# Reordering the activation slab by time then channel in a two-layer spatio-temporal network on one core

## The reference

```
x_res = conv2d(swapaxes(x, 1, 2), res_w, res_b)
xc = swapaxes(_attention(swapaxes(x, 1, 2), W1_c, W2_c, True), 1, 2)    # over channels
xt = swapaxes(_attention(swapaxes(xc, 1, 3), W1_t, W2_t, True), 1, 3)   # over times
s  = _attention(xt, W1_s, W2_s, False)                                  # over nodes
h  = einsum('bnm,bmct->bnct', s * A[None], xt)
g  = einsum('bnct,cf->bnft', h, W_gcn)
y  = relu(conv2d(swapaxes(g, 1, 2), tcn_w, tcn_b, pad 1) + x_res)
z  = (y - mean over channels) / sqrt(var + 1e-05) * ln_g + ln_b
```

## Time and profile before

| | us |
|---|---|
| median of 3 runs | 2099.84 |
| span of the profiled execution | 2096.6 |
| PE busy | 1603.6 (76%) |
| DVE busy | 1216.3 (58%) |
| ACT busy | 716.1 (34%) |
| POOL busy | 489.9 (23%) |

### The profile page before, as it was taken

The page is one execution under the profiler, slowest core; times in us unless marked ns, Lnnn a source line. Parts: engine busy times, 40 slices in busy tenths (PEclk is TensorE's granted clock), DMA queues, the critical chain, the costliest instruction groups (busy, mean ns, idle before and its releaser), DMA issues. The chain is left out here.

```text
span 2096.6 us, 28757 instructions
## 1 busy us (share of the span) xinstructions
PE 1603.6 (76%) x8438; PEld 1232.3 (59%) x8438; DVE 1216.3 (58%) x2496; ACT 716.1 (34%) x1145; POOL 489.9 (23%) x854
## 2 busy tenths in 40 slices
PE   4589799999655279999999333788999999147776
PEld 4439577777433168888888233276777777135554
DVE  4511277787645844444444377121677877658986
ACT  3302144434334033333332122021344344047775
POOL 1100033443501231111110365000234434201111
PEclk7599799999879579999999655888999999579988
DMA  6403012212156133333331777033122111012322
GB/s 198 118 17 104 23 46 60 68 53 60 46 173 197 42 117 117 117 116 116 116 117 43 221 237 228 15 111 103 33 61 63 57 60 49 27 48 81 90 76 67
DMA packets 151973, 193.44 MB, mean 92 GB/s; under 512 B 11657, under 2 KB 103273, under 8 KB 151917
## 3 DMA queue, kind: packets, MB, share of 16 engines
q1 hardware_dynamic: 101021, 116.46, 19.0%
q10 hardware_dynamic: 41680, 47.96, 7.3%
q0 software_dynamic: 9216, 28.32, 4.5%
HBM read 126.64 MB, written 66.06 MB: 92 GB/s over the span
## 5 line engine op out<-in xcount | busy, mean ns | idle before, releaser
L701 PE MATMUL g_y<-L_z,L_pt 128*128 128x192 f32 x1024 | 188.6, 327 | 0.3 <-ACT L_pt L917 0.2
L909 ACT ACTIVATE L_e<-g_s,L_nm 128x512 f32<-128x512 f32 x128 | 88.0, 687 | 287.1 <-DVE L_nm L745 286.3
L701 PEld LDWEIGHTS g_y<-L_z,L_pt 128*128 128x128 f32 x1024 | 170.8, 190 | 1.2 <-ACT L_pt L917 1.2
L865 POOL TENSOR_TENSOR L_xr<-L_xr,L_lnb 128x192 f32<-128x192 f32 x128 | 84.8, 690 | 306.1 <-DMA L_xr<-x 159.9
L1193 POOL DMA_INDIRECT x_xin<-xn_rows,x_index x64 | 66.3, 1036 | 295.3 <-PE ex_t L1207 146.8
L872 POOL TENSOR_TENSOR L_t<-L_rstd 128x48 f32<-128x48 f32 x96 | 35.6, 371 | 320.1 <-DVE L_rstd L806 315.1
L668 PE MATMUL g_z<-L_kw,L_xnT 96*128 96x192 f32 x512 | 95.8, 341 | 15.1 <-DVE L_v L775 15.1
L1287 DVE TENSOR_TENSOR x_mid<-ex_g,x_sig 128x480 f32<-128x480 f32 (+1 forms) x48 | 31.4, 654 | 122.4 <-ACT x_sig L1362 122.4
L668 PEld LDWEIGHTS g_z<-L_kw,L_xnT 96*128 96x128 f32 x512 | 86.5, 196 | 27.0 <-DVE L_v L775 27.0
L754 DVE SCALAR_TENSOR_TENSOR L_p<-L_e,L_rl,L_adj 128x512 f32<-128x512 f32 x128 | 96.4, 753 | 4.7 <-DVE L_rl L752 0.3
L745 DVE TENSOR_REDUCE L_nm<-g_s 128x1 f32<-128x512 f32 x128 | 87.9, 686 | 13.4 <-PE g_s L677 7.9
(11 more groups left out here) (267 smaller groups left out, 4005.5 us busy)
## 6 DMA issues: line engine op xcount, KB each, us to landing
xn_rows<-L_xnT SPq DMA_DIRECT2D x48, 384.0 KB, 3.8
L_xnT<-xn_rows SPq DMA_DIRECT2D x48, 384.0 KB, 3.4
y_slots<-x_yo ACTq DMA_DIRECT2D x64, 240.0 KB, 2.4
x<-L_y ACTq DMA_DIRECT2D x32, 384.0 KB, 3.2
L_xa<-in_x SPq DMA_DIRECT2D x16, 384.0 KB, 4.1
L_raw<-xn_rows SPq DMA_DIRECT2D x16, 384.0 KB, 3.4
L_xr<-in_x SPq DMA_DIRECT2D x16, 384.0 KB, 3.3
L_xa<-x SPq DMA_DIRECT2D x16, 384.0 KB, 4.0
```

Source lines behind the costliest of these rows:

```text
L701: last = nc.tensor.matmul(out, pt[k % 2][:, P * c:P * c + P], z[q][:, c, :], start=False, stop=(c == NK - 1))
L865: last = nc.gpsimd.tensor_tensor(v_, v_, gain(s.lnb), ALU.add)
L909: nc.scalar.activation(e[k % 2][:, :], pss[k % 2][:, :], ACT.Exp, bias=s.nm2[:, k % 2:k % 2 + 1], accum_out=s.l[:, k % 2:k % 2 + 1]).then_ ...
```

## The change

All slabs are ordered by time, then channel: a column is time * 16 + channel. The host lays x out so before the launch, and the kernel writes its output back in the old order. In parts:

1. `small_attention` reads contiguous columns for both attentions. The channel fold becomes the same for both halves (one matmul and one copy where there were two), the time fold differs (two matmuls and one copy twice as wide).
2. `mix_channels` has one 96 x 96 block for both halves. Each of the 8 matmuls of an item has 96 columns and doesn't accumulate. It writes its half in channel-time order, as the time attention wants it.
3. `graph_conv`: the residual weights are 96 columns wide, so the two matmuls have 97 rows and 96 columns each; the projections have 96 weight columns; `u` and `v` have 128 rows, cleared by four DVE operations at the start of the stage; the slab copy goes from DVE to ACT, where it stands ahead of the exponential; the sums over channels read contiguous elements; POOL's four operations with `ln_b` and four with `ln_g` are one each.
4. `route` counts in the old token order: six matmuls for each choice instead of two, running sums over 16 items instead of 32 half items, and one more addition.
5. `feed_forward` writes its sum to new buffers `yo` in channel-time order; the wait for an earlier store moves from DVE's product to POOL's addition.
6. `conv_weights` and the constants follow the new order (masks per half, 96 columns of residual weights, ones for both halves).

```diff
@@ small_attention
-    xa = s.shared[:, 0:B * NK * CT].rearrange("p (b k c t) -> p b k c t", b=B, k=NK, c=C)
+    xa = s.shared[:, 0:B * NK * CT].rearrange("p (b k x w) -> p b k x w", b=B, k=NK, w=W)
...
-                        rhs = xa[:, :, k, :, x] if chan else xa[:, :, k, x, :]
-                        last = nc.tensor.matmul(psp[0:PROJ, 0:n_all], w[:, k, x, :], rhs,
+                        last = nc.tensor.matmul(psp[0:PROJ, 0:n_all], w[:, k, x, :], xa[:, :, k, x, :],
                                                 start=(j == 0), stop=(j == n - 1))
@@ mix_channels
-                        for h in range(2):
-                            last = nc.vector.tensor_tensor(
-                                big[z % 2][0:HALF, h, :].rearrange("p (c t) -> p c t", t=T),
-                                s.rct[0:HALF, h, bass.ds(b * C, C)].unsqueeze(2).to_broadcast([HALF, C, T]),
-                                s.tmask[:, 1, :].unsqueeze(1).to_broadcast([HALF, C, T]), ALU.mult)
-                        last.then_inc(big_done, 1)
+                        nc.vector.tensor_tensor(
+                            big[z % 2][0:HALF, 0, 0:HALF].rearrange("p (c t) -> p c t", t=TH),
+                            s.rct[0:HALF, bass.ds(b * C, C)].unsqueeze(2).to_broadcast([HALF, C, TH]),
+                            s.tmask[:, 0, 1, 0:TH].unsqueeze(1).to_broadcast([HALF, C, TH]),
+                            ALU.mult).then_inc(big_done, 1)
...
-                                last = nc.tensor.matmul(psm[z % 2][:, k // 2, CT * (k % 2):CT * (k % 2) + CT],
-                                                        xnT[z][0:HALF, h, P * k:P * k + P], big[z % 2][0:HALF, h, :],
-                                                        start=(h == 0), stop=(h == 1))
+                                last = nc.tensor.matmul(
+                                    psm[z % 2][:, k // 2, CT * (k % 2):CT * (k % 2) + CT].rearrange(
+                                        "p (c t) -> p c t", t=T)[:, :, TH * h:TH * h + TH],
+                                    xnT[z][0:HALF, h, P * k:P * k + P],
+                                    big[z % 2][0:HALF, 0, 0:HALF].rearrange("p (c t) -> p c t", t=TH),
+                                    start=True, stop=True)
@@ graph_conv
-        oct_ = lambda t: t[:, :, :].rearrange("p k (o t) -> p k o t", t=T)
-        lanes = lambda t: t.unsqueeze(2).to_broadcast([P, NK, O, T])
-        gain = lambda t: t[:, :].rearrange("p (o x) -> p o x", x=1).to_broadcast([P, O, T])
+        oct_ = lambda t: t[:, :, :].rearrange("p k (t o) -> p (k t) o", o=O)
+        flat = lambda t: t[:, :, :].rearrange("p k t -> p (k t)")
+        lanes = lambda t: flat(t).unsqueeze(2).to_broadcast([P, NK * T, O])
+        gain = lambda t: t[:, :].unsqueeze(1).to_broadcast([P, NK * T, O])
...
-                        last = nc.tensor.matmul(psz[0:NPROJ, 1, :], kw[q][0:HALF, h, 0:NPROJ], xnT[q][0:HALF, h, :],
+                        last = nc.tensor.matmul(psz[0:HALF, 1, :], kw[q][0:HALF, h, 0:HALF], xnT[q][0:HALF, h, :],
...
-                    nc.tensor.matmul(pss[k % 2][:, :], u[q][0:KR, P * k:P * k + P], v[q][0:KR, :],
+                    nc.tensor.matmul(pss[k % 2][:, :], u[q][:, P * k:P * k + P], v[q][:, :],
...
-                    nc.tensor.matmul(out, xnT[q][0:HALF + 1, 0, P * k:P * k + P], s.res[0:HALF + 1, 0, :],
-                                     start=True, stop=False)
-                    nc.tensor.matmul(out, xnT[q][0:HALF, 1, P * k:P * k + P], s.res[0:HALF, 1, :],
-                                     start=False, stop=False)
+                    for h in range(2):
+                        nc.tensor.matmul(out[:, HALF * h:HALF * h + HALF], xnT[q][0:HALF + 1, h, P * k:P * k + P],
+                                         s.res[0:HALF + 1, h, :], start=(h == 0), stop=False)
...
+                for padded in (*u, *v):
+                    nc.vector.memset(padded[:, :].bitcast(F32), 0.0)
...
-                def copy_z(b, q):
-                    dve.wait_ge(z_done, ready(b))
-                    dve.wait_ge(y_done, free(b, 2))
-                    nc.vector.tensor_copy(slab(z[q]), psz[:, :, 0:2 * CT]).then_inc(z_sb, 1)
...
-                    step(nc.vector.tensor_reduce(s.mu[:, :, :], y[q][:, :, :].rearrange("p k (o t) -> p k t o", t=T),
-                                                 AX, ALU.add))
+                    step(nc.vector.tensor_reduce(flat(s.mu), oct_(y[q]), AX, ALU.add))
...
-                        copy_z(b + 1, r)
                         row_max(b + 1, 0)
...
-                        for k in range(NK):
-                            v_ = dv[q][:, k, :].rearrange("p (o t) -> p o t", t=T)
-                            last = nc.gpsimd.tensor_tensor(v_, v_, gain(s.lng), ALU.mult)
-                        last.then_inc(gained, 1)
+                        nc.gpsimd.tensor_tensor(oct_(dv[q]), oct_(dv[q]), gain(s.lng), ALU.mult).then_inc(gained, 1)
...
+                def copy_z(b, q):
+                    act.wait_ge(z_done, ready(b))
+                    act.wait_ge(y_done, free(b, 2))
+                    nc.scalar.activation(slab(z[q]), psz[:, :, 0:2 * CT], ACT.Copy).then_inc(z_sb, 1)
...
                     if project:
+                        copy_z(b + 1, r)
                         row_exp(b + 1, 0)
@@ feed_forward
-                        nc.gpsimd.tensor_tensor(ya[q][:, :, :], ya[q][:, :, :], xr[q][:, :, :],
-                                                ALU.add).then_inc(out_done, 1)
+                        in_time = lambda t: t[:, :, :].rearrange("p k (t c) -> p k t c", c=C)
+                        pool.wait_ge(sent[q], dma_free(i))
+                        nc.gpsimd.tensor_tensor(yo[q][:, :, :].rearrange("p k (c t) -> p k t c", t=T),
+                                                in_time(ya[q]), in_time(xr[q]), ALU.add).then_inc(out_done, 1)
```

More of the change, by code:

```diff
@@ L36 @@
 HALF = CT // 2
+TH = T // 2
 TILES = B * 2
@@ L204, in _ @@
                 dve.wait_ge(mix_done, 1)
                 for h in range(2):
[L206 to L210, removed]
+                    rows = lambda x, n: x.unsqueeze(1).to_broadcast([HALF, n, O])
@@ L459, in _ @@
                         pe.wait_ge(turned_sb, g + 1)
-                        for h in halves:
-                            last = nc.tensor.matmul(psf[g][0:HALF, 256 + n_half * h:256 + n_half * h + n_half],
-                                                    fold(h), s.spt[0:n_half, g, 0:n_half], start=True, stop=True)
+                        last = nc.tensor.matmul(psf[g][0:HALF, 256:256 + n_half], fold(0),
+                                                s.spt[0:n_half, g, 0:n_half], start=True, stop=True)
                     last.then_inc(folded, 1)
@@ L987, in sb @@
             return ctx.enter_context(nc.sbuf_tensor("r_" + name, shape, dt))
[L989 removed]
+        iota, tri, logits = sb("iota", [HALF, E]), sb("tri", [HALF, 2, 2, HALF]), sb("logits", [HALF, G])
         key, gate, cand, left = (sb(n, [HALF, TILES, E]) for n in ("key", "gate", "cand", "left"))
         hot = [sb("hot0", [HALF, TILES, E]), sb("hot1", [HALF, TILES, E])]
[L992 removed]
+        tot, run, place = sb("tot", [HALF, B, E]), sb("run", [HALF, B, E]), sb("place", [HALF, TILES, E])
         top, idx, gval, rank, keep = (sb(n, [HALF, TILES]) for n in ("top", "idx", "gval", "rank", "keep"))
[L994 removed]
+        ones = sb("one", [HALF, B])
         tokens = sb("tokens", [HALF, 2, TILES])
@@ L1041, in _ @@
                     pe.wait_ge(chosen, c + 1)
-                    nc.tensor.matmul(pre[c][0:HALF, 0:G], tri[:, :], flat(hot[c]), start=True, stop=True)
-                    nc.tensor.matmul(all_[c][0:HALF, 0:G], s.ones[0:HALF, 0:HALF], flat(hot[c]), start=True,
-                                     stop=True).then_inc(counted, 1)
+                    part = lambda f: hot[c][:, :, :].rearrange("p (b h) e -> p h b e", h=2)[:, f, :, :]
+                    for h in range(2):
+                        for f in range(2):
+                            nc.tensor.matmul(
+                                pre[c][0:HALF, 0:G].rearrange("p (b h e) -> p h b e", h=2, e=E)[:, h, :, :],
+                                tri[:, f, h, :], part(f), start=(f == 0), stop=(f == 1))
+                    for f in range(2):
+                        last = nc.tensor.matmul(all_[c][0:HALF, 0:B * E].rearrange("p (b e) -> p b e", e=E),
+                                                s.ones[0:HALF, 0:HALF], part(f), start=(f == 0), stop=(f == 1))
+                    last.then_inc(counted, 1)
                 for c in range(2):
@@ L1838, in product @@
                     dve.wait_ge(down_done, ready(b))
-                    dve.wait_ge(sent[q], dma_free(i))
+                    dve.wait_ge(out_done, free(b, 2))
                     for a in range(2):
```

134 lines of the change are left out of this document (71 added, 63 removed).

## The result

The changed kernel takes 2150.73 us (median of 4 runs, 2150.41 to 2153.70) against 2099.97 for the kernel before; the ratio is 1.0245, 95% interval 1.023 to 1.0259. The forecast was 2082 with a range of 2035 to 2120. The time went the other way, and beyond the third rival's 2125.

The account below looks back on a forecast made before the run. No engine bounds the whole; in spatial attention's loop engines hand work round, and DVE leads the last stage. Terms −41 + 18 + 4 − 27 + 17 + 3 − 2 + 11 − 1 = −18 gave 2082 us, range 2035 to 2120.

Parts of the forecast that it names:

- third rival: Spatial attention: PE's new waits drop the clock in nearly every item, 2.0 lost each; slower, 2125 us, chance 0.17.
- Channel projections: Channel attention: contiguous reads bring records from 0.446 to 0.217 us apart, 22.3 against 42.8 a layer; −41 us in two.
- The rival by which the change doesn't do what it says: Channel attention: records keep 0.446 us although contiguous, 256 columns into one bank being the cause; 2123 us, chance 0.03.
- Mix: Mix stage: 96-column records stay at the low clock, 0.213 us apart, 54.7 instead of 45.5 a stage; +18 us.
- first rival: Mix: the clock rises there after all, −47 us for it and −4 for the time projections; 2031 us, chance 0.12.
- Time projections, cleared operands: Time attention starts at the low clock, +4 us; four operands cleared at the start of a layer, +3 us.
- the second of spatial attention: Spatial attention's LN sums: contiguous reads cut each from 1.52 to 0.95 us, shortening the item by 0.2 (bounds 0 and −0.56).
- The price: Spatial attention: PE waits 2.1 us before the projections, so the clock falls in half the items; +17 us (0 to +33).
- The slab copy's move: Spatial attention: with the slab copy on ACT, DVE's row maximum starts earlier, −0.69 us an item.
- Padding the scores: Spatial attention: 128-row operands save PE about 0.3 us for each of four scores, which gains nothing by itself.
- POOL's strided write in the last stage: Last stage: POOL's addition writing every 48 bytes delays DVE by 0.7 us, sixteen times; +11 us (0 to +29).
- The rest: Channel and time folds, routing's extra matmuls, half-length scans and addition, longer loads of ones: −1 us (−4 to +2).

## Why the prediction was wrong

- **Channel projections**: right. 22.6 us against the forecast 22.3, and the run with the stride alone confirms it. The rival by which the change doesn't do what it says is out.
- **Mix**: right in size (56.2 a stage; forecast 54.7 for the records, and they take 54.9) and in its mechanism, that no rise comes. What the forecast left out is that the same records hold the level where they find it. The first rival was wrong for this kernel, and names what the change missed.
- **Time projections, cleared operands**: 9.3 against 7. The four clearings follow one another by 0.52, 2.1 a layer.
- **The step that failed** is the second of spatial attention: "as one operation of about 1.8 it still ends at about 410.4, where the centring now ends at 411.37. I take −0.2 (bounds 0 and −0.56)". It counted one of POOL's operations, the multiplication, and set it beside the centring's old end. But with the sum over channels shorter, the mean is due while the multiplication runs; and right behind the multiplication stands the addition of `ln_b`, now 1.81 without a gap as well, which the centring has to wait out. In the trace before, the addition's first quarter stood there (the earlier trace rows leave it out), and DVE lost 0.1 to it:

```profile
410.52 2.63 POOL L865 TENSOR_TENSOR L_xr<-L_xr,L_lnb 128x192 f32<-128x192 f32 x4
```

The stretch grew by 1.6 an item instead of shrinking by 0.2. Over thirty items that is some 55 of the 72 us. With POOL split it measures 3.5, as the forecast had it (3.79 − 0.2), and items with the high level last 18.95 (forecast 19.05). So the step was right for the change without its merged operations, and its bounds lacked the side of a loss: one operation of 1.8 us in place of four of 0.5 was costed as a gain.
- **The price** was right as a mechanism and wrong in its input. It said 2.1 of wait and half of the items at 1.1. The wait was 3.6, for the port's 1.6 came on top; 22 of 30 items fell, and the mean item, those that didn't fall included, lost 1.4. Over the 26 items measured that is 36 us instead of 17, most of what is left of the 72. With POOL split the wait is only 1.74 and 2 of 30 items fall, 0.15 an item on average: there the 17 us were far too much. At a wait of 2.25, the run with the copy on DVE shows 15 of 30 items, the forecast's half; at 2.4 (only the addition split) it is 12, at 2.0 to 2.1 (POOL's operations merged in the kernel before) 10.
- **The slab copy's move**: the forecast said −0.69, the run shows 0.45 while the clock is high, and 38 us in all, for the move also keeps PE's wait short.
- **Padding the scores** was said to gain nothing by itself. It gains up to 15 us with POOL split, 0.45 in an item at the high level: a score that ends earlier lets DVE begin its row maximum earlier. If the parts add up, copy and padding are the whole of the 0.9 an item (19.85 to 18.95) and the sums over channels gain about nothing, where the forecast had 0.69 and 0.2. So the total was right by luck, by errors that cancel.
- **POOL's strided write in the last stage**: wrong. The addition, which now writes every 48 bytes, takes 1850 ns on average against 1834 in the same group of the kernel before (one of them is in the earlier trace rows), so the cost is 0.016 an item instead of 0.7, and the stage is 1.6 us longer instead of 11. No row of before had such a write, and the value came from DVE's reads; the Trainium skill, "GPSIMD Engine Reference" (§ 7), states its cost for reads alone, and the trace shows none for this write.

```profile
L1898 POOL TENSOR_TENSOR ff_yo<-ff_ya,ff_xr 128x768 f32<-128x768 f32 x16 | 29.6, 1850 | 139.0 <-DVE ff_ya L1852 139.0
```

- **The rest**, as far as it lies between the layers, is 5.4 longer instead of about as long. 3.3 of it lie between the second normalisation and the first expert's work, where routing has more matmuls than before; the cause was not followed further and stays open.
- **The sums**: the bounds that the forecast names for falls and for POOL's write give 2054 to 2117 by plain addition, not 2060 to 2112. And every execution with both figures has its time 1.8 us above its span (2150.98 and 2149.2), so the 3.2 taken for what lies outside was 1.4 too much. Neither changes the direction of the forecast.

The slower rival ended on the right side and was given 0.17, but its cause, falls alone, was less than half of the loss: 1.4 an item, beside the port's 1.7.

## What to carry to other kernels

When small operations of POOL become one large one, ask which short operation of DVE slips in between them today, and which POOL operation stands next in POOL's own queue: here DVE got in between the parts and not between the merged ones. When an engine off the path is made faster, its wait grows; if that engine is TensorE, read the clock behind the wait before the saving is booked, and price filling the wait with useless matmuls, which here paid 29 us. Before a stage of short matmuls, look at the level at which it starts: here six to eight us of streaming ahead of it, most of them spent in a wait for a load anyway, were worth 22 to 24 us a layer.

## What the runs showed that I had not expected

- The same 256 records of 96 columns run at 0.50 for 54.9 us or at 1.00 for 28.8, after what PE did before them.
- POOL and DVE pass the port on between operations, not within one: POOL's four quarters take 2.95 us with DVE in between, 1.81 as one; DVE's one-input mean of 48 elements waited as well, 0.98 instead of 0.19.
- More projections fall with a longer wait ahead of them, though not strictly: at waits of 1.03 (before) 1 of 30 items, the one whose wait was 1.30; at 1.18 none, 1.74 two, 2.05 ten, 2.25 fifteen, 2.4 twelve, 3.6 twenty-two.
- A POOL operation over [128, 768] takes 1.50 us where the gain is broadcast along the inner 12 elements and 1.81 where it is read along the inner 16; the reason was not looked for.
